# A two-stack macaron kernel on one core: the slots of each stack written out on every engine, in place of a loop over 16 tiles

## The reference, cut to what matters

```python
def stack(x):
    for l in range(6):
        x = x + attn_layer(shift_tokens(layernorm(x)), Wqkv[l], ...)
        x = x + ffn_layer(x, W1[l], W2[l], ...)
def attn_layer(x, Wqkv, qs, ksc, Wo):
    q, k, v = split(x @ Wqkv)                     # 16 heads of 64
    q, k = l2norm(q) * qs, l2norm(k) * ksc        # then a rotary rotation with a scale
    # a window of 32 queries sees its own 32 keys and the 32 before
    return softmax(8 * q @ k.T + mask) @ v @ Wo
def ffn_layer(x, ...):
    a, gate = split(layernorm(x) @ W1 + b1)       # 341 wide each
    return a * gelu(gate) @ W2 + b2
```

## Time and profile before

| what | value |
|---|---|
| median of the runs | 3688.96 us |
| the profiled execution's own time | 3686.52 us |
| its span in the profile | 3684.7 us |
| PE busy | 3433.7 us (93%) |
| DVE, ACT, POOL busy | 77%, 65%, 63% |
| DMA, mean over the span | 23 GB/s |
| granted TensorE clock, mean | 0.97 |

### The profile page before, as it was taken

How to read it: one execution, slowest core, us unless ns; L and a number is a source line. 1 busy time by engine, 2 the same in 40 slices (tenths; PEclk the granted TensorE clock), 3 DMA queues, 4 the chain that set the end, 5 groups by cost and what they waited for, 6 DMA issues and landing times.

```text
span 3684.7 us, 129395 instructions
## 1 busy us (share of the span) xinstructions
PE 3433.7 (93%) x51660; PEld 1855.8 (50%) x51660; DVE 2845.5 (77%) x6042; ACT 2381.3 (65%) x4153; POOL 2333.4 (63%) x2187
## 2 busy tenths in 40 slices
PE   3799999999999999999797999999999999999997
PEld 2355554554554554555363555545545545545553
DVE  1788887887887887888367888878878878878883
ACT  1576776775776776677524667767767766766774
POOL 0677766766766776767145767667667766767661
PEclk6899999999999999999998999999999999999999
DMA  5000000000000000000100000000000000000000
GB/s 187 10 9 28 21 12 27 22 12 27 21 13 27 21 12 25 24 12 5 54 1 8 11 26 23 12 27 21 13 27 21 12 27 22 12 24 26 12 5 13
DMA packets 50151, 83.62 MB, mean 23 GB/s; under 512 B 7168, under 2 KB 37120, under 8 KB 47232
## 3 DMA queue, kind: packets, MB, share of 16 engines
q1 hardware_dynamic: 49536, 75.05, 6.5%
HBM read 67.69 MB, written 7.34 MB: 20 GB/s over the span
## 4 chain that ended last, share of the span: by engine, by line
PE 86%; issue 4%; DVE 4%; ACT 3%; POOL 1%; DMA 1%; SPq 0%; DVEq 0%; ACTq 0%; POOLq 0%
PE VS L890 19%; PE QA L830 18%; PE TB L849 10%; PE TB L914 7%; PE VS L937 7%; PE TB L873 6%; PE FB L963 3%; PE FB L964 3%; PE FB L972 3%; PE VS L928 2%; ACT KT L460 2%; PE TB L857 1%; PE FB L948 1%; PE FB L953 1%; DMA KT<-in_w_out 1%
## 5 line engine op out<-in xcount | busy, mean ns | idle before, releaser
L334 POOL TENSOR_TENSOR QN<-T 128x512 f32<-128x512 f32 x768 | 980.0, 1276 | 673.6 <-DVE T L606 673.6
L341 POOL TENSOR_TENSOR QN<-QN,RR 128x512 f32<-128x512 f32 x768 | 801.6, 1044 | 316.8 <-DVE RR L627 316.8
L830 PE MATMUL QA<-WQ,Y 128*128 128x512 f32 x1536 | 806.3, 622 | 68.7 <-DVE T L606 25.4
L890 PE MATMUL VS<-MW,Y 128*32 128x512 f32 x6144 | 738.8, 598 | 2.7 <-DVE Z L679 2.7
L446 ACT ACTIVATE SQ<-QA 128x512 f32<-128x512 f32 x768 | 458.6, 597 | 289.3 <-PE QA L830 254.5
L606 DVE TENSOR_TENSOR T<-QA,TAB 128x256 f32<-128x256 f32 x1536 | 571.0, 412 | 4.1 <-issue 4.1
L601 DVE TENSOR_TENSOR T<-QA,TAB 128x512 f32<-128x512 f32 x768 | 522.9, 681 | 48.2 <-issue 21.3
L466 ACT ACTIVATE V<-VS 128x512 f32<-128x512 f32 x768 | 461.1, 600 | 90.1 <-PE VS L890 89.5
L633 DVE TENSOR_TENSOR Y<-TB,Y 64x128 f32<-64x128 f32 x384 | 111.0, 289 | 521.0 <-PE TB L857 518.3
L614 DVE TENSOR_REDUCE SSQ<-SQ 128x8 f32<-128x512 f32 x768 | 486.8, 675 | 0.0
L914 PEld LDWEIGHTS TB<-CST,QN 128*128 128x128 f32 x3072 | 360.9, 142 | 220.9 <-issue 183.5
(11 more groups left out here) (172 smaller groups left out, 4260.2 us busy)
## 6 DMA issues: line engine op xcount, KB each, us to landing
TAB<-in_tables SPq DMA_DIRECT2D x192, 128.0 KB, 2.1
WQ<-in_w_qk SPq DMA_DIRECT2D x48, 256.0 KB, 3.2
MW<-m_dram SPq DMA_DIRECT2D x12, 1024.0 KB, 4.8
m_dram<-QN SPq DMA_DIRECT2D x6, 1024.0 KB, 4.9
W1R<-in_w SPq DMA_DIRECT2D x12, 341.0 KB, 3.4
KT<-in_w_vt SPq DMA_DIRECT2D x6, 512.0 KB, 5.8
KT<-in_w_out SPq DMA_DIRECT2D x6, 512.0 KB, 6.6
W<-in_w SPq DMA_DIRECT2D x12, 192.0 KB, 2.4
```

The costliest lines, as they stand in the source:

```text
L334: po.tensor_tensor(QN[:, n % 2, k, :], T1[:, k, :], T2[:, k, :], ALU.add).then_inc(s_add, 1)
L341: po.tensor_tensor(heads(QN[:, m % 2, k, :]), heads(QN[:, m % 2, k, :]), RR[:, m % 2, 8 * k:8 * k + 8].unsqueeze(2).to_broadcast([P, 8, DH ...
L830: mm(QA[:, k % 2, :], Y[:, j * P:(j + 1) * P], WQ[:, k, :], start=True, stop=True).then_inc(s_qk, 1)
L890: last = mm(VS[32 * q:32 * q + 32, w % 2, :], Y[:, a:a + WIN], MW[:, q, :], start=True, stop=True, tile_position=(0, 32 * q), skip_group_c ...
```

## The change

The loop is taken out, and all 104 slots of a stack are written out on each of the five engines. `it` is then always `None`, so each wait asks for a constant, and each weight load has a constant address. SP finds the layer from the slot's number, and the slots that loaded weights in the loop still load them. TensorE's `edge` keeps its meaning: only the first and the last 12 slots have the additional waits. Each engine does the same arithmetic and the same transfers in the same order.

```diff
@@ all_slots
-            for c in range(AHEAD):
-                slot(c, None, s)
-            with engine.Fori(0, DEPTH - 1) as it:
-                for c in range(AHEAD, AHEAD + TPL):
-                    slot(c, it, s)
-            for c in range(AHEAD + TILES - TPL, LAST):
+            for c in range(LAST):
                 slot(c, None, s)
@@ SP, slot
-                if it is None:
+                if not AHEAD <= c < AHEAD + TILES - TPL:
                     return
-                nxt = bass.ds(it + 1, 1)
-                if c == AHEAD:
-                    sp.wait_ge(s_w1, by_layer(1, s * DEPTH, it, 1))
-                    sp.wait_ge(s_prb, by_layer(1, s * DEPTH, it, 1))
+                l = (c - AHEAD) // TPL + 1
+                nxt = slice(l, l + 1)
+                if c % TPL == AHEAD:
+                    sp.wait_ge(s_w1, by_layer(1, s * DEPTH + l - 1, it, 1))
+                    sp.wait_ge(s_prb, by_layer(1, s * DEPTH + l - 1, it, 1))
                     up_weights(nxt)
@@ TensorE, slot
-                edge = it is None
+                edge = c < AHEAD or c >= AHEAD + TILES - TPL
```

## The result

The changed kernel takes 3640.94 us, the median of 4 runs (3630.2 to 3646.27), against 3689.6 us of before (4 runs, 3684.85 to 3692.18) on the same chip: a ratio of 0.9866 (its 95% interval, here and below in brackets, is [0.9838, 0.9893]). The forecast of 3649 us, 1.1% faster, holds. The profiled execution took 3636.46 us, with a span of 3634.7 us: 50.0 us less than the 3684.7 us of before.

What follows compares the result with a forecast made beforehand. PE, busy for 93% of the span, was taken to bound the kernel. Profiled 3686.5 - 71.0 (turns) + 30.6 (stalls) = 3646.1 us, stated as a 3649 us median, 1.1% faster; range 3614 to 3674 us.

Steps and rivals of the forecast that it cites:

- The turns, -71.0 us: Eight slot pairs around loop turns shrink from 43 to 46 us to the branch-free (clean) pairs' 35.5 us: 71.0 us saved.
- The register arithmetic goes. I cost it at nothing.: Sequencers' register instructions, about 32 ns each, vanish; PE's matmuls already cover them, so 0 us gained.
- the plain slots stay at 16.05 us: Sign: plain slots take 16.05 us in the loop and written out, and keep that length after the change.
- The long code, +30.6 us: In PE's scores, late instruction packets cause 18 new stalls at 1.7 us each: 30.6 us lost.
- 5 in 16: Share of written-out slots with c % 4 = 3 or 0 that stalled before; over 80 such slots, 25 stalls.
- all in slots with c % 4 = 3 or 0: Sign: stalls in PE's scores, 12 to 30 in number, come only where no up-projection stands before the mask.
- one placement repeated: The two loop bodies' 16 exposed slots show no stall, but each is a single code placement that is only repeated.
- straight code streams for nothing: Rival, 0.18: the edge slots' additional waits cause the five stalls; new slots lack them, so none is added: 3618 us.
- eleven edge slots with the same waits don't stop: Argument against additional waits as the cause: eleven of sixteen edge slots of the same kind have them without a stall.
- The other signs: Line 201 without instructions, no 2.8 us VectorE "issue" at turns, PE packets under 431, SP's constant addresses costing nothing.
- handed on: Rival, 0.06: the turns' 71 us come back as waits on VectorE or DMA; time stays about 3689 us.
- each exposed slot stalls: Rival, 0.06: all 80 slots without an up-projection before the scores stall 1.7 us, 136 us in all: 3754 us.

Runs made afterwards that it cites:

- experiments 2 and 3: Changed kernel with the loop brought back on all engines but PE: 3675.73 us; with the loop brought back on PE alone: 3656.34 us.
- Experiments 9 to 11: KT's wait put ahead of s_ve's in the changed kernel's middle slots, 3615.39 us; ahead of all the mask's waits in kernel 10, 3563.08 us, and kernel 11, 3596.28 us.
- kernel 11: Changed kernel with KT's wait put ahead of all other waits before the mask, edge slots included: 3596.28 us, ratio 0.9752.
- experiment 4: Changed kernel with the first 16 token transposes done three times, shifting PE's later code by 64 instructions: 3654.88 us, ratio 0.9901.
- kernel 9: Changed kernel with KT's wait put ahead of the wait for s_ve before the mask, in slots 12 to 91 of a stack: 3615.39 us.
- experiment 6: Changed kernel with feed-forward work (centring, last down-projection) moved from before the transposes to between them and the mask: 3597.86 us, and 3598.33 us when repeated.
- kernel 10: Kernel of experiment 6 with KT's wait put ahead of all other waits before the mask: 3563.08 us, ratio 0.9658.

## Why the prediction was right, and where its steps failed

*The turns, -71.0 us.* Right, to 1.3 us: every former turn is a clean pair but for new stops, at a clock of 1.00, and 69.7 us were measured. That PE's branch and the others' add up on the path is shown by experiments 2 and 3, with 47 us for PE's and 22 us for the others'.

*"The register arithmetic goes. I cost it at nothing."* Wrong by 7.5 us, to the good. The 32 ns are indeed nothing (slots with c % 4 = 1 take 15.97 us in the loop and with constants); but the price was looked for in the arithmetic's length only. Its place mattered: on ScalarE it held a wait ahead of a table load. The row that told of it, ten waits of PE for QT, was there in the waits of the kernel before, and the prediction did not ask why only the loop had them. The statement that the plain slots stay at 16.05 us missed the mask's 0.09 us too.

*The long code, +30.6 us.* The mechanism was right, packets that come too late in the scores. The term was too high by 11 us, which is most of the difference between the forecast and the result: 12.4 us came in the scores and 6.9 us in the transposes behind them. That 20 stops stand in the row, where 5 + 18 = 23 were forecast, is luck. The kind that was forecast, long stops in newly written-out slots with c % 4 = 3 or 0, came 7 times in place of 18, at 1.6 us each (and 4 times, at 1.0 to 1.3 us, in the transposes behind the scores), so the price of 1.7 us was right and the count was not: 5 in 16 was a small sample. The stops that fill up the row are of kinds that were not foreseen: 0.4 to 0.8 us, in slots with c % 4 = 1 and 2 (0:29 0.45 us, 0:30 0.44, 1:22 0.77), and edge slots at new places (1:5 1.53 us, 1:95 1.58). So "all in slots with c % 4 = 3 or 0" was wrong, and so was its reason, that the up-projections let the sequencer run ahead in the others: the separate wait held it in all 191 slots.

*Why the loop had none.* The prediction took it for one placement repeated. Experiments 9 to 11 show a cause that is enough without it: the loop's 160 slots carry KT's wait in the weight load, the edge slots in a separate instruction, and with constants all do; in straight code with KT's wait back in the load (kernel 11) one stop is left in the middle slots. A loop with KT's wait in an instruction of its own was not run, so for the loop itself this is argued. Placement (experiment 4) only picks the slots that pay. So the rival "straight code streams for nothing" named the better half of the cause, the waits of the edge slots, and erred in that the new slots would not have them. That its 3618 us is near kernel 9's 3615 us is chance: the one knows nothing of the wait for QT, and the other still has stops. The argument held against it, that eleven edge slots with the same waits don't stop, is what placement does.

*What the Trainium skill says.* The Trainium skill (Runtime: NRT & Kernel Launch, Instruction fetch mechanics) has it that crossing a 16 KiB block is mostly hidden and that a taken branch to code outside the blocks at hand stalls. The traces agree about the size (6.73 MB / 411 = 16.4 KB) and the branch (4.22 us), and in kernel 11 about the crossing (3 stops in the scores, 1.8 us). In the changed kernel they differ: a crossing costs up to 1.9 us if the sequencer was held just before a burst of dense code.

*The mask's wait, +7.3 us.* Not in the sum at all. It went from 0.28 to 0.35 us apiece over 102 times; with KT's wait in the weight load again (kernel 11) it is 0.27 us. So it has the same cause as the stops. It cancels the wait for QT to 0.2 us by chance, so the total is better than its parts.

*The other signs.* Line 201 is gone, VectorE no longer has "issue" of 2.8 us in the turns, packets fall from 431 to 411, SP and its addresses cost nothing that can be seen. The rivals "handed on" and "each exposed slot stalls" are out: no new wait for another engine stands in the former turns, and 30 stops are far from 80 of 1.7 us.

*What is left open.* Whether the loop would also gain from experiment 6 was not tried, so of kernel 10's 126.6 us (3689.71 - 3563.08) only the order of the waits (3598 - 3563 = 35 us) and the moved work (3596 - 3563 = 33 us) are priced by themselves.

## What to carry to other kernels

When a loop is written out, look at more than its turns: a wait with a constant and one with a register's value can end up in other instructions, and here this gained 7.5 us through ScalarE and cost 26.6 us (12.4 + 6.9 + 7.3) on PE. Where several semaphores are waited for ahead of a dense burst, put the one that comes last first in the code, so that it sits in the work itself and not in an instruction that holds the sequencer; one moved line was worth 45 us (3640.94 to 3596.28), almost as much as the change. And an "issue" stop within straight code is a reason to look at when the instruction packet came.

## What the runs showed of the hardware that was not expected

The order of two waits on one matmul decides how far PE's sequencer may run ahead. With the late one in the weight load, a packet began to come 0.6 to 0.8 us ahead of the mask; in a separate instruction, 1.0 to 1.2 us after it (slot 0:48), with 2.2 to 2.6 us from the packet's start to PE's next matmul in 13 stops. A separate wait also delays the matmul itself by 0.09 us (0.34 against 0.25 us in slot 0:48, and in the other middle slots with c % 4 = 0 or 3). And setting four full transposes between two halves of the small-tile scores made PE busy for 0.35 us more a slot, with the same matmuls.
